# Routing of layer one: from a stage of its own into the loop of context attention, in a two-layer decoder on one Trainium2 core

## Chip, cores and metric

One NeuronCore of one Trainium2 chip. The metric is the device time of one execution in microseconds (us). TensorE (PE; its weight loads are PEld), VectorE (DVE), ScalarE (ACT), GpSimd (POOL) and SyncE (SP, which only issues transfers) run their own instruction streams and wait for each other on semaphores.

## The reference, cut to what matters

A decoder of two layers on x (16 sequences of 112 tokens, width 256) and a context (16 x 375 x 256). Each layer is self-attention, attention to the context and a mixture of experts, each added to x. The part in question is the routing of layer one, on the normalised output of its context attention:

```python
x = x + _L1_xattn_ref(_layernorm(x), ctx_1024, ...)      # 8 heads of 64, 375 context tokens
x = x + _L1_ffn_ref(_layernorm(x), ...)
# in _L1_ffn_ref, for each sequence (Tt = 112, E = 8, K = 2, cap = 33):
logits = jnp.einsum('btc,ce->bte', x, router_w) + router_b
top_k_logits, expert_indices = jax.lax.top_k(logits, K)
expert_probs = jax.nn.softmax(top_k_logits, axis=-1)
ei = jnp.swapaxes(expert_indices, 0, 1).ravel()          # all first choices, then all second ones
one_hot = jax.nn.one_hot(ei, E, dtype=jnp.int32)
pos = jnp.cumsum(one_hot, axis=0) * one_hot - 1          # the rank of a token within its expert
buf = jnp.zeros((E, expert_capacity, Cc), x.dtype)
expert_inputs = buf.at[ei.ravel(), pos.ravel()].add(xr)  # out of the capacity: dropped
# then silu(h * g) @ w_c_proj per expert, and each token collects its two outputs by expert_probs
```

## The kernel before, in words

`decoder` runs the stages one after another: `linear_attention`, `add_and_norm`, `context_attention_0`, `experts_0`, `self_attention_1`, `context_attention_1`, `experts_1`. Each is a block in which every engine has its own program; between blocks the engines meet, and a finished stage clears its semaphores.

`context_attention_1` (line 1888) works a sequence at a time. Turn i of all engines' loops does the attention of sequence i, whose heads come in two groups of four: scores, maximum (DVE, L2060), exponentials (ACT, L2004), transposes of the probabilities (PE, L2219), their copy out of PSUM (DVE L2066 and ACT L2010 in turn), the products with the values (PE, L2236). Between these main steps stand side steps, which prepare the sequences ahead (context two turns ahead; keys, values, queries one ahead) and finish the one behind (`result`, `rows`). A table, `side = Side([...])`, gives each a sequence offset and one of two PSUM banks, one emptied by ACT and one by DVE, and the order of the table is that of TensorE and of the engine that empties the bank. Each engine's order is written out in its `iteration`; no scheduler changes it. `sequences_ahead` runs turns -3 to 0 unrolled, 1 to 12 in a loop of two turns, 13 to 16 unrolled. DVE normalises the rows of sequence i - 1 in turn i (`rows_ready`, L2097) and writes them a second time to `XN` (L2098); `rows` transposes them to `xnT`.

`experts_1` (line 2275) then has four blocks. The first routes all sequences at once: 32 router matmuls (L2318), the two best experts by `top_two` on DVE, ranks by products with an upper triangle of ones (L2323 to L2325), probabilities, positions; SP loads the weights of experts 0 and 1. The second makes for each sequence, on DVE, the one-hot matrix of its 8 x 33 slots, and multiplies the rows with it in fp32 (L2424) to `ex`, the expert inputs, already transposed. The third is the experts' work: weights and inputs are split in a high and a low fp32r half (ACT rounds, L2486; GpSimd subtracts, L2475) and multiplied in three products (`split_products`). The fourth combines.

`experts_0` works through BLOCKS = 44 tiles of 128 rows, which hold every distribution of 3584 rows over 16 experts padded to tiles.

## Time and profile before

| | |
|---|---|
| median of 3 runs | 1944.72 us (1944.21 to 1952.29) |
| the profiled execution | 1952.73 us |
| its span, first to last instruction | 1951.1 us |
| mean granted clock of TensorE | 0.946 of full |
| busy: PE, DVE, ACT, POOL | 1719.9, 1177.2, 828.2, 452.9 us |
| context attention of layer one, first scores to the last rows | 1184.1 to 1552.6 us |
| routing and slots | 1552.6 to 1609.0 us |
| experts of layer one | 1609.0 to 1901 us |

The span is the time of one execution between its first and last instruction; the rest of the 1952.73 lies around it. Times in rows count from the span's start. In a timeline row, "[0.36 <-PE ps L1215]" says that the engine had been idle for 0.36 us and what ended that. "x8" merges neighbouring instructions; an fp32 matmul shows as two records, an fp32r one as one.

### The profile page before, as it was taken

What the parts mean: (1) busy time and instruction counts of PE and PEld (TensorE: products, weight loads), DVE (VectorE), ACT (ScalarE), POOL (GpSimd) and SP (SyncE); (2) the same over time, 40 slices, a digit from 0 to 9 for tenths busy, and PEclk for the clock granted to TensorE, in tenths of its full rate; (3) what the DMA queues carried; (4) which work ended last, traced back from release to release, by engine and by line L of the source; (5) the groups of instructions that cost most, each with busy time, mean ns of one, the idle gap of its engine ahead of it and who ended that gap; (6) DMA issues with size and microseconds to landing.
All of it is one profiled execution on the core that took longest, in us unless ns stands there. A gap on an engine that the chain in (4) does not pass through costs nothing. (4 is left out here: it accounts for less than half of the span.)

```text
span 1951.1 us, 39011 instructions
## 1 busy us (share of the span) xinstructions
PE 1719.9 (88%) x13070; PEld 1375.2 (70%) x13070; DVE 1177.2 (60%) x2667; ACT 828.2 (42%) x2420; POOL 452.9 (23%) x710
## 2 busy tenths in 40 slices
PE   3887689999998687799999949999999759999998
PEld 2555456666666476688888837777787649999996
DVE  3887546777777443366666534666665365666657
ACT  1332345555555123244444424444444245554534
POOL 1111201222222222212112021111111006544523
PEclk9999789999999699799999969999999879999999
DMA  8000133333350433000000000000000122312101
GB/s 241 0 0 0 55 93 125 119 123 123 123 171 11 151 119 120 20 11 13 11 9 12 4 24 24 17 16 16 21 10 1 40 90 70 126 66 93 37 1 38
DMA packets 87656, 114.20 MB, mean 59 GB/s; under 512 B 4832, under 2 KB 77071, under 8 KB 87311
## 3 DMA queue, kind: packets, MB, share of 16 engines
q1 hardware_dynamic: 82382, 99.91, 16.0%
q0 software_dynamic: 5184, 13.11, 2.0%
q8 instruction: 54, 0.88, 0.2%
q14 instruction: 36, 0.29, 0.1%
HBM read 65.04 MB, written 47.97 MB: 58 GB/s over the span
## 5 line engine op out<-in xcount | busy, mean ns | idle before, releaser
L1215 PE MATMUL ps<-e_ex_high,e_w_high 128*128 128x264 f32 x512 | 146.8, 287 | 5.4 <-POOL e_w_low L2475 5.4
L1215 PE MATMUL ps<-e_ex_high,e_w_low 128*128 128x264 f32 x512 | 146.5, 286 | 0.0
L1215 PE MATMUL ps<-e_ex_low,e_w_high 128*128 128x264 f32 x512 | 146.2, 286 | 0.0
L931 ACT ACTIVATE c_probs<-ps,c_negmax 112x375 f32<-112x375 f32 x256 | 143.7, 581 | 2.1 <-DVE c_negmax L1028 2.1
L1028 DVE TENSOR_REDUCE c_negmax<-ps 112x2 f32<-112x750 f32 x128 | 114.2, 934 | 34.7 <-PE ps L1152 34.7
L1814 PE MATMUL ps<-xnT,s_qkv 128*128 (+1 forms) x1024 | 130.5, 285 | 2.0 <-DVE xnT L1661 1.0
L1121 PEld LDWEIGHTS ps<-const,c_probs 112*125 112x125 f32 x768 | 99.0, 193 | 45.3 <-DVE c_pT L1044 19.4
L1814 PEld LDWEIGHTS ps<-xnT,s_qkv 128*128 128x128 f32 x1024 | 123.2, 199 | 6.4 <-DVE xnT L1661 1.7
L1628 ACT ACTIVATE s_probs<-ps,s_negmax 112x112 f32<-112x112 f32 x256 | 86.7, 365 | 74.8 <-DVE s_negmax L1677 74.8
L1121 PE MATMUL ps<-const,c_probs 112*125 112x112 f32 x768 | 115.1, 287 | 3.5 <-DVE c_pT L1044 2.0
L2004 ACT ACTIVATE c_probs<-ps,c_negmax 112x375 f32<-112x375 f32 x128 | 71.7, 574 | 83.1 <-DVE c_negmax L2060 83.1
L1215 PEld LDWEIGHTS ps<-e_ex_high,e_w_high 128*128 128x128 f32 x512 | 97.6, 191 | 5.8 <-issue 5.8
L1215 PEld LDWEIGHTS ps<-e_ex_high,e_w_low 128*128 128x128 f32 x512 | 97.6, 191 | 0.0
L1215 PEld LDWEIGHTS ps<-e_ex_low,e_w_high 128*128 128x128 f32 x512 | 97.5, 190 | 0.0
L2475 POOL TENSOR_TENSOR e_w_low<-e_wgt,e_w_high 128x256 fp32r<-128x256 f32 x64 | 49.0, 766 | 175.4 <-ACT e_w_high L2486 175.4
L2495 ACT ACTIVATE xnT<-ps,columns 128x528 f32<-128x528 f32 x64 | 45.0, 703 | 99.6 <-PE ps L1215 99.6
L2536 DVE SCALAR_TENSOR_TENSOR xnT<-ps,columns,xnT 128x528 f32<-128x528 f32 x64 | 49.0, 766 | 60.4 <-PE ps L1215 60.4
L919 ACT COPY c_pT<-ps 125x672 f32<-125x672 f32 x64 | 46.0, 719 | 84.2 <-PE ps L1121 84.2
L2542 DVE CAST e_hid_high<-xnT 128x528 fp32r<-128x528 f32 x64 | 45.3, 708 | 58.1 <-ACT xnT L2501 47.7
L2060 DVE TENSOR_REDUCE c_negmax<-ps 112x2 f32<-112x750 f32 x64 | 57.1, 934 | 36.0 <-PE ps L2207 34.2
L1215 PE MATMUL ps<-e_hid_high,e_w_high 128*128 128x264 f32 x256 | 73.6, 287 | 5.9 <-DVE e_ex L2523 4.2
L2219 PE MATMUL ps<-const,c_probs 112*125 112x112 f32 x384 | 65.8, 281 | 7.9 <-DVE c_pT L2066 3.1
(361 smaller groups left out, 4600.2 us busy)
## 6 DMA issues: line engine op xcount, KB each, us to landing
expert_rows<-d_zero SPq DMA_DIRECT2D x16, 2240.0 KB, 12.1
c_ctx_in<-in_ctx SPq DMA_DIRECT2D x32, 375.0 KB
e_wgt<-in_L_ffn_w_gate SPq DMA_DIRECT2D x8, 1024.0 KB, 5.0
e_wfc<-in_L_ffn_w_c_fc SPq DMA_DIRECT2D x8, 1024.0 KB, 7.2
e_wpj<-in_L_ffn_w_c_proj SPq DMA_DIRECT2D x8, 1024.0 KB, 9.6
e_x_in<-expert_rows SPq DMA_DIRECT2D x44, 128.0 KB, 2.0
expert_rows<-e_y POOLq DMA_DIRECT2D x44, 128.0 KB, 2.0
s_qkv<-in_L_attn_W_qkv SPq DMA_DIRECT2D x1, 3072.0 KB, 11.2
```

What stands on the lines that cost most here:

```text
L919: nc.scalar.copy(pT[:, 2:4, :], ps[:KC, BANK_PT:BANK_PT + 2, 0:SC]).then_inc(pT_ready, 1)
L931: last = nc.scalar.activation(probs[:, g % 2, r, :], ps[:T, r, 0:S], ACT.Exp, bias=negmax[:, par, h:h + 1], accum_out=sums[:, par, h:h + 1])
L1028: nc.vector.tensor_reduce(negmax[:, par, h:h + 3:2], ps[:T, 2 * piece:2 * piece + 2, 0:S], AX.X, ALU.max, negate=True).then_inc(max_done, 1)
L1121: last = nc.tensor.transpose(ps[:KC, BANK_PT + r % 2, k * T:(k + 1) * T], probs[:, g % 2, r, k * KC:(k + 1) * KC], ident[:T, :T])
L1215: last = nc.tensor.matmul(out, a, b, start=start and n == 0, stop=stop and n == len(pairs) - 1)
L1628: last = nc.scalar.activation(probs[:, j, a, :], ps[:T, BANK_S + j, a * T:(a + 1) * T], ACT.Exp, scale=0.125, bias=negmax[:, h:h + 1], acc ...
L1814: last = nc.tensor.matmul(bank[:, u4 * T:(u4 + 1) * T], wv[:, c, j, n * 128:(n + 1) * 128], sh.xnT[:, c, i + 1, :], start=(c == 0), stop=( ...
L2004: nc.scalar.activation(probs[:, x, :], ps[:T, x, 0:S], ACT.Exp, scale=0.125, bias=negmax[:, h:h + 1], accum_out=sums[:, h:h + 1]).then_inc ...
L2060: nc.vector.tensor_reduce(negmax[:, h:h + 2], ps[:T, 2 * pair:2 * pair + 2, 0:S], AX.X, ALU.max, negate=True).then_inc(max_done, 1)
L2219: last = nc.tensor.transpose(ps[:KC, BANK_PT, k * T:(k + 1) * T], probs[:, x, k * KC:(k + 1) * KC], ident[:T, :T])
L2475: last = nc.gpsimd.tensor_tensor(low, whole, high.bitcast(F32), ALU.subtract)
L2536: nc.vector.scalar_tensor_tensor(ubuf[:, j % 2, :, :], ps[:, 0:2, 0:HALF], sh.columns[:, bass.ds(n_all, 1)], gbuf[:, :, :], ALU.add, ALU.m ...
```

## The change

The routing of layer one moves into the turns of `context_attention_1`. A class `Dispatch1` holds its steps; q is the sequence:

- turn q + 1: DVE normalises the rows once (`dispatch.xn`; `XN` is gone), casts their high half (`keep_high`), GpSimd makes the low half (`keep_low`). `rows` becomes `rows_ranks`, stands earlier (after the first transposes of group 1) and copies to `own`; `inverse` becomes `inverse_logits` and has the router's two matmuls behind it.
- turn q + 2: best two experts (`take_best`, `mark_experts`), GpSimd keeps the two best values; the rank products behind the row transposes of the next sequence in `rows_ranks`; DVE masks them (`take_ranks`) and selects slots (`select_slots`); GpSimd builds the one-hot matrix in fp32r (`one_hot`: two multiplications and an addition on 112x264).
- turn q + 3: the side steps `slots0` and `slots1`, behind the scores of either group, each two fp32r matmuls of 264 columns (high and low half of the rows); ACT copies to `ex`.

`sequences_ahead` now unrolls turns -3 to 4, loops over 5 to 12, and unrolls 13 to 19. The first two blocks of `experts_1` are gone. Expert 0's weights are loaded at the start of the attention on SP, behind the first two context loads; expert 1's at the start of the experts' block. The probabilities are computed in the third piece of the experts (ACT's exponential ahead of the first). BLOCKS becomes 43. The rest makes room in SBUF: `self_attention_1` keeps its tiles in the memory of layer zero's expert weights, and tiles that only the start of the kernel needs are freed before `context_attention_0`.

```diff
-BLOCKS = 2 * ROWS // TILE + E0
+BLOCKS = (2 * ROWS - E0) // TILE + E0
...
-    for i in range(-ahead, 1):
+    start = 5 if behind else 1
+    for i in range(-ahead, start):
...
+class Dispatch1:
...
+    def take_best(self, dve, q, u, taken):
...
+        self.link(dve, q, 1, nc.vector.max(self.best[:, u, :], self.values[:, :]))
+        nc.vector.max_index(self.best_at[:, :], self.best[:, u, :], self.values[:, :]).then_inc(self.best_ready, 1)
...
+    def mark_experts(self, dve, q):
...
+        self.link(dve, q, 2, nc.vector.tensor_copy(self.chosen[:, :], self.best_at[:, 0:2]))
+        nc.vector.tensor_tensor(self.sh.hot[:, q, :, :], mid(self.sh.c("expert_ids")[:T, 0:E1], 2), bc(self.chosen[:, :], E1),
+                                ALU.is_equal).then_inc(self.hot_ready, 1)
...
+    def rank_products(self, pe, bank, q):
+        nc = self.nc
+        pe.wait_ge(self.hot_ready, q + 1)
...
+    def select_slots(self, dve, q, taken):
...
+        self.link(dve, q, 3, nc.vector.tensor_reduce(self.sh.slot[:, q, :], self.ranks[:, :, :], AX.X, ALU.add))
...
+            last = nc.vector.tensor_scalar(self.sel[:, k, :], self.sh.c("slots")[:T, :], self.sh.slot[:, q, k:k + 1], None, ALU.is_equal)
...
+    def slot_products(self, pe, bank, q, u, c):
+        nc = self.nc
+        pe.wait_ge(self.oneh_ready, q + 1)
+        pe.wait_ge(self.low_ready, q + 1)
+        for n, part in enumerate((self.xn_high, self.xn_low)):
...
-    side = Side([("result", -1, ON_DVE), ("query", 1, ON_ACT), ("key0", 1, ON_DVE), ("context0", 2, ON_ACT),
-                 ("key1", 1, ON_DVE), ("key2", 1, ON_ACT),
-                 ("key3", 1, ON_DVE), ("value0", 1, ON_ACT), ("value1", 1, ON_DVE), ("context1", 2, ON_ACT),
-                 ("rows", -1, ON_DVE), ("inverse", 0, ON_DVE), ("value2", 1, ON_ACT)])
+    side = Side([("slots0", -3, ON_ACT), ("result", -1, ON_DVE), ("query", 1, ON_ACT), ("key0", 1, ON_DVE), ("context0", 2, ON_ACT),
+                 ("key1", 1, ON_DVE), ("key2", 1, ON_ACT), ("slots1", -3, ON_ACT),
+                 ("key3", 1, ON_DVE), ("rows_ranks", -1, ON_DVE, B + 1), ("value0", 1, ON_ACT), ("value1", 1, ON_DVE),
+                 ("context1", 2, ON_ACT), ("inverse_logits", 0, ON_DVE, B + 1), ("value2", 1, ON_ACT)])
...
+            load_expert(sh, sp, e1, 0, 0, e1.even)
...
-                nc.vector.tensor_scalar(sh.XN[:, i - 1, :], x, ln.mv[:T, 0:1], ln.rstd[:T, :], ALU.subtract, ALU.mult)
...
+                if within(i - 2):
+                    dispatch.mark_experts(dve, i - 2)
                 maxima(i, 1)
+                if within(i - 1):
+                    dve.wait_ge(xn_ready, i)
+                    dispatch.keep_high(dve, i - 1, 1 - par, slots_used(i))
                 evacuate("key3", i, par)
                 copy_probs(i, 1, 0)
+                evacuate("rows_ranks", i, par)
                 context_statistics(i + 3, 1 - par)
+                if within(i - 2):
+                    dispatch.select_slots(dve, i - 2, (side_done[ON_DVE], side.done("rows_ranks", i)))
                 inverse_sums(i)
                 evacuate("value1", i, par)
                 copy_probs(i, 1, 2)
-                evacuate("rows", i, par)
-                evacuate("inverse", i, par)
+                evacuate("inverse_logits", i, par)
...
+                load_expert(sh, sp, w, 1, 1, w1)
...
+                        if is_first and n == 2:
+                            probabilities()
```

VectorE, from the copy of the last keys to the copy that frees the last transposes. Before, in the loop, where rows that set registers (REGISTER_ALU, ISA) stand among the others:

```order
L2112 BN_AGGR c_ctx_mean_var<-c_ctx_stats 125x2 x3
L80 REGISTER_ALU
L2114 TENSOR_SCALAR c_ctx_var_eps<-c_ctx_mean_var 125x3
L2070 ISA
L2071 RECIPROCAL c_inv<-c_sums 112x8
L2073 COPY c_inv_wide<-c_inv 112x512
L2040 ISA
L2049 COPY c_v<-ps 125x512
L2065 REGISTER_ALU
L2066 COPY c_pT<-ps 125x336
```

Now, in turn 4, which is unrolled:

```order
L1966 CAST d_xn_high<-d_xn 112x256
L2191 COPY c_kT<-ps 128x375
L2206 COPY c_pT<-ps 125x336
L2185 COPY d_own<-ps 128x224
L1948 TENSOR_TENSOR d_ranks<-ps,hot 112x16
L2246 BN_STATS c_ctx_stats<-c_ctx_in 125x6 x3
L2252 BN_AGGR c_ctx_mean_var<-c_ctx_stats 125x2 x3
L2254 TENSOR_SCALAR c_ctx_var_eps<-c_ctx_mean_var 125x3
L1955 TENSOR_REDUCE slot<-d_ranks 112x2
L1960 TENSOR_SCALAR d_sel<-const,slot 112x33 x2
L2211 RECIPROCAL c_inv<-c_sums 112x8
L2213 COPY c_inv_wide<-c_inv 112x512
```

The copy of the transposed rows and the masking of the ranks stand ahead of the context statistics now, and the reduction and the two selections between the statistics and the sums; `c_v` and `c_pT` follow as before.

TensorE, from the second last transposes of group 1 to the last side step. Before, in turn 13 (`c_probs` are the probabilities, `c_cn` the context, `c_xn` the rows, `c_inv_wide` the inverse sums):

```order
L2219 MATMUL ps<-const,c_probs 125x112 x3
L2182 MATMUL ps<-const,c_cn 128x125 x3
L2172 MATMUL ps<-const,c_xn 128x112 x2
L2219 MATMUL ps<-const,c_probs 125x112 x3
L2163 MATMUL ps<-const,c_inv_wide 128x112 x4
```

Now, in turn 4:

```order
L2377 MATMUL ps<-const,c_probs 125x112 x3
L2340 MATMUL ps<-const,c_cn 128x125 x3
L2377 MATMUL ps<-const,c_probs 125x112 x3
L2314 MATMUL ps<-const,c_inv_wide 128x112 x4
L1911 MATMUL ps<-e_router,d_own 112x8 x2
```

The row transposes have gone from between the last two groups of transposes (they stand ahead of the values now, with the rank products behind them), and the router's matmuls follow the inverse sums.

## Rows read from the trace of the kernel before

**Rows 1.** Engine windows: stretch, its length, busy of PE, PEld, DVE, ACT, POOL, granted clock, DMA share, GB/s.
```profile
1206.41:1229.20 22.79, 22.55 (x168) 18.03 (x168) 14.53 (x33) 10.74 (x28) 4.01 (x5) 1.00 0.06 19
...
1548.00:1567.00 19.00, 14.36 (x74) 13.47 (x74) 2.60 (x8) 0.00 (x0) 0.55 (x1) 0.64 0.63 226
```

**Rows 2.** Timeline of one loop turn: start us, us, engine, line, operation [idle before <-releaser].
```profile
1400.11 1.52 PE L2207 MATMUL ps<-c_kT,c_qT 64*112 64x375 f32 x8
...
1401.56 0.44 PE L1215 MATMUL ps<-c_ctx_high,c_kv_high 128*128 128x376 f32 x1
...
1402.74 0.40 PEld L2219 LDWEIGHTS ps<-const,c_probs 112*125 112x125 f32 x3 [0.19 <-ACT c_probs L2004]
...
1403.78 1.07 DVE L2106 BATCH_NORM_STATS2 c_ctx_stats<-c_ctx_in 125x6 f32<-125x256 f32 x3
...
1405.45 0.20 DVE L2071 RECIPROCAL c_inv<-c_sums 112x8 f32<-112x8 f32 x1
...
1406.48 0.69 DVE L2049 COPY c_v<-ps 125x512 f32<-125x512 f32 x1 [0.36 <-PE ps L1215]
...
1407.09 0.50 DVE L2066 COPY c_pT<-ps 125x336 f32<-125x336 f32 x1
...
1407.73 0.55 PE L2219 MATMUL ps<-const,c_probs 112*125 112x112 f32 x3
...
1422.90 1.52 PE L2207 MATMUL ps<-c_kT,c_qT 64*112 64x375 f32 x8
```

**Rows 3.** Timeline, from the loop's last rows to the first expert matmul.
```profile
1552.19 0.41 DVE L2097 TENSOR_SCALAR c_xn<-X,c_mean_var,c_rstd 112x256 f32<-112x256 f32 x1 [0.66 <-POOL c_rstd L113]
...
1553.17 0.39 DVE L2047 COPY xnT<-ps 128x224 f32<-128x224 f32 x1 [0.24 <-PE ps L2172]
...
1554.48 12.08 PE L2318 MATMUL ps<-e_router,xnT 128*112 128x8 f32 x64 [1.35 <-PEq L98]
...
1574.60 0.39 DVE L2380 TENSOR_SCALAR e_sel<-const,e_pos 112x33 f32<-112x33 f32 x2 [0.53 <-PEq L2307]
...
1603.68 0.67 ACT L2404 COPY e_ex<-ps 128x264 f32<-128x264 f32 x2 [0.86 <-PE ps L2424]
...
1604.70 0.40 ACT L2486 CAST e_w_high<-e_wgt 128x256 fp32r<-128x256 f32 x1 [0.35 <-PEq L2387]
...
1609.02 0.56 PE L1215 MATMUL ps<-e_ex_high,e_w_high 128*128 128x264 f32 x1 [5.38 <-POOL e_w_low L2475]
```

**Rows 4.** Timeline, GpSimd and VectorE side by side, layer one and layer zero.
```profile
1405.60 0.87 POOL L1949 TENSOR_TENSOR c_ctx_rstd<-c_ctx_var_eps,const 125x3 f32<-125x3 f32 x1 [6.54 <-DVE c_ctx_var_eps L2114]
...
1405.69 0.43 DVE L2073 COPY c_inv_wide<-c_inv 112x512 f32<-112x512 f32 x1
...
342.20 0.23 DVE L712 TENSOR_SCALAR d_hot<-const,d_chosen 112x16 f32<-112x16 f32 x1
...
657.59 0.73 POOL L729 TENSOR_TENSOR X<-X,d_xn 112x256 f32<-112x256 f32 x1
...
657.86 0.50 DVE L712 TENSOR_SCALAR d_hot<-const,d_chosen 112x16 f32<-112x16 f32 x1 [0.15 <-DVE d_chosen L711]
```

**Rows 5.** Timeline of TensorE: layer zero's gate and ranks, expert matmuls.
```profile
560.96 0.56 PE L649 MATMUL ps<-e_gate,d_own 128*112 128x16 f32 x4 [0.38 <-DVE c_v L976]
...
561.57 0.35 PE L654 MATMUL ps<-d_totals,const 112*112 112x16 f32 x2
...
1616.02 0.28 PE L1215 MATMUL ps<-e_ex_high,e_w_low 128*128 128x264 f32 x1
...
1616.14 0.29 PE L1215 MATMUL ps<-e_ex_high,e_w_high 128*128 128x264 f32 x1
```

**Rows 6.** Timeline of TensorE in the experts of layer zero, two blocks.
```profile
702.43 0.59 PE L1473 MATMUL ps<-e_down,e_hidT 128*128 x2
...
704.06 0.59 PE L1473 MATMUL ps<-e_down,e_hidT 128*128 x2
```

**Rows 7.** Page, DMA issues: operation, count, KB each, us to landing.
```profile
e_wpj<-in_L_ffn_w_c_proj SPq DMA_DIRECT2D x8, 1024.0 KB, 9.6
```

More of the change, by code:

```diff
@@ L44, in constant_columns @@
     put("count16", np.tile(np.arange(16, 0, -1), (T, 1)))
-    put("slots", np.tile(np.arange(CAP), (T, 1)))
+    put("slots", np.tile(np.arange(1, CAP + 1), (T, 1)))
     put("upto", np.triu(np.ones((T, T))))
@@ L1491, in __init__ @@
     def __init__(self, steps):
-        self.steps = steps
-        self.bank = {name: u for name, _, u in steps}
-        self.offset = {name: offset for name, offset, _ in steps}
+        self.steps = [step if len(step) == 4 else step + (B,) for step in steps]
+        self.bank = {name: u for name, _, u, _ in self.steps}
+        self.offset = {name: offset for name, offset, _, _ in self.steps}
+        self.times = {name: times for name, _, _, times in self.steps}
     def present(self, name, i):
-        return within(i + self.offset[name])
+        k = i + self.offset[name]
+        return not isinstance(k, int) or 0 <= k < self.times[name]
     def before(self, name, i):
         total, later = 0, 1
-        for other, offset, u in self.steps:
+        for other, offset, u, times in self.steps:
             if other == name:
@@ L1516, in within, with sequences_ahead, self_attention_1 @@
     return not isinstance(q, int) or 0 <= q < B
-def sequences_ahead(eng, ahead, iteration):
-    for i in range(-ahead, 1):
+def sequences_ahead(eng, ahead, iteration, behind=0):
+    start = 5 if behind else 1
+    for i in range(-ahead, start):
         iteration(i, i % 2)
-    with eng.Fori(1, B - 4, 2) as i:
+    with eng.Fori(start, B - 4, 2) as i:
         iteration(i, 1)
         iteration(i + 1, 0)
-    for i in range(B - 3, B + 1):
+    for i in range(B - 3, B + 1 + behind):
         iteration(i, i % 2)
-def self_attention_1(nc, sh, w):
+def self_attention_1(nc, sh, w, spare):
     H, DH, HALF = 16, 64, 4 * T
@@ L2159, in aside @@
                     pe.wait_ge(side_done[u], taken)
-                if name == "inverse":
-                    pe.wait_ge(inv_ready, i + 1)
-                    for c in range(4):
-                        last = nc.tensor.transpose(bank[:, c * T:(c + 1) * T],
-                                                   inv_wide[:, 2 * c:2 * c + 2, :].rearrange("p h d -> p (h d)"), ident[:T, :T])
+                if name == "inverse_logits":
+                    if within(i):
+                        pe.wait_ge(inv_ready, i + 1)
+                        for c in range(4):
+                            last = nc.tensor.transpose(bank[:, c * T:(c + 1) * T],
+                                                       inv_wide[:, 2 * c:2 * c + 2, :].rearrange("p h d -> p (h d)"), ident[:T, :T])
+                    if within(i - 1):
+                        last = dispatch.logits(pe, logits_at)
                 elif name == "result":
@@ L2354, in experts_1 @@
+        ex = sh.ex
+        held = sb("held", [T, B, 2])
+        prob = sb("prob", [T, 2, B])
+        diff = sb("diff", [T, B])
+        diff_ready, ediff_ready, chain = sem("diff_ready"), sem("ediff_ready"), sem("chain")
+        w1 = ExpertWeights(lambda name, shape: sb(name + "_odd", shape))
+        weights, w_in = (w.even, w1), w.w_in
         sel = sb("sel", [T, 2, CAP])
@@ L2359, in experts_1 @@
         spare = lambda at, n: flat_xnT[:, at:at + n]
-        own = spare(10 * HALF, 2 * D)[:T].rearrange("p (u d) -> p u d", u=2)
         def sequences(eng, step):
@@ L2526, in take_outputs, with probabilities @@
                     last.then_inc(out_taken, 1)
+                def probabilities():
+                    link = chained(dve, chain, 0)
+                    nc.vector.tensor_scalar(held[:, :, :], sh.slot[:, :, :], float(CAP), None, ALU.min)
+                    dve.wait_ge(ediff_ready, 1)
+                    link(nc.vector.tensor_scalar(prob[:, 0, :], prob[:, 1, :], 1.0, None, ALU.add))
+                    link(nc.vector.reciprocal(prob[:, 0, :], prob[:, 0, :]))
+                    link(nc.vector.tensor_tensor(prob[:, 1, :], prob[:, 1, :], prob[:, 0, :], ALU.mult))
                 def pair(e2, is_first, is_last):
```

334 lines of the change are left out of this document (177 added, 157 removed).

## The prediction

> **What bounds the kernel now.** The chain of waits that ended last reaches back only into the combining of the outputs, so I read the stages instead: the engine windows for context attention of layer one, the timeline for what follows it, and the timeline of one turn of the loop. In the loop TensorE is busy 22.55 of 22.79 us, at the full granted clock [rows 1]; one sequence takes 22.79 us, from second scores to second scores (1400.11 to 1422.90) [rows 2]. TensorE is the bound, but inside the turn it waits for VectorE in one place: between 1403.78 and 1407.59 VectorE works almost without a gap (statistics, sums, copy of values, copy of probabilities), and the transposes of the last head start at 1407.73, when that last copy is there [rows 2]. After the loop comes the stage the change is about. The last normalised rows are finished at 1552.60 (1552.19 + 0.41), the first real expert matmul starts at 1609.02 [rows 3]. In these 56.4 us nothing overlaps with attention: 64 router matmul records, top-two, ranks, and 16 small slot products; TensorE's granted clock is 0.64 in the first 19 us of it [rows 1].
>
> **What goes.** All of these 56.4 us as a stage of its own. What replaces them is a tail: the last sequence's router, ranks and slots still hang behind its rows. Laid end to end from 1552.60: rank products of sequence 14, copy of the own rows, logits, best two, marking: about 4 us, since these are small instructions of 0.2 us on VectorE [rows 4] and pairs of 0.2 to 0.4 us on TensorE [rows 5], which at half clock take twice that. TensorE then stands before the slots of sequence 14, which wait for GpSimd's one-hot (three instructions on 112x264; its 112x256 add took 0.73 [rows 4], so 2.3 with the hand-overs), then twice product and ScalarE copy (0.4 each; a pair of 264-column copies took 0.67 [rows 3]): about 3.8 us. Then ranks, selection (1.5), one-hot (2.3) and two products with copies (1.9) of sequence 15. Sum 13 to 13.5 us; bounds 10 (sequence 14 hidden entirely) and 18 (every hop at half clock, GpSimd held). I take 13. Behind it stay the way from one block to the next with the clearing of semaphores, 0.9 (after the loop's last copy, to the router's first matmul, an estimate: the row copy ended at 1553.56, and the router began at 1554.48 [rows 3]), and the splitting of the first expert piece, 4.3 (1604.70 to 1609.02 [rows 3]). New stage 18.2 us; gain 38.2.
>
> One block less in the experts of layer zero (43 for 44): the same matmul group starts at 702.43 and 704.06, so 1.6 us [rows 6]. The stage of layer zero is a chain of such blocks on TensorE, so all of it counts.
>
> **What the loop gains in work, TensorE.** Per sequence: logits, two fp32 matmuls of 8 columns; layer zero's gate and ranks with 16 columns are the nearest, three of them from 560.96 to 561.57, so 0.20 each [rows 5] and 0.40 for the pair. Ranks, two more: 0.40. Slot products, now four fp32r matmuls of 264 columns: 0.12 each (1616.02 to 1616.14) [rows 5], 0.50, in two pairs. Together 1.3 us on an engine that has 0.24 to spare in 22.79. The row transposes only move.
>
> **What the loop gains in waits, VectorE.** The order fence shows what now stands ahead of the copy that TensorE waits for: the copy of the own rows (about 0.4; 0.50 was for 336 columns [rows 2]), the masking of the ranks (0.2), their reduction (0.2), two selections (0.39 for two [rows 3]). The write of XN falls away, but it stood where VectorE waited for the scores anyway; best two and marking sit in such gaps too, and the high half of the rows is cast while TensorE makes the last keys. So these cost nothing, and if that cover were gone each would cost 0.2 to 0.5 per turn. With 0 at the start of the second scores (1400.11), after the change: TensorE has scores to 1.45 (1401.56), slots to 1.70, keys to 2.73 (1.18 less the 0.19 that the next transposes waited [rows 2]), transposes at 2.93 (the slot copy stands 0.35 ahead of the exponentials on ScalarE), rows and ranks from 3.65 (they wait for the copy of the keys, about 0.5 like the other copies) to 4.27; VectorE has rows and ranks out at 5.1, statistics at 6.8 (1.67, from 1403.78 to 1405.45), selection 7.45, sums 8.1, values 8.8, probabilities 9.3; TensorE resumes at 9.4, where before it did at 7.62 (1407.73) [rows 2]. That is +1.78. Logits add 0.40, the first slot pair 0.25, and a hand-over of some 0.1 goes, since the inverse transposes no longer wait for the row copy. One turn grows by 2.3 us, to 25.1. Bounds: 1.3 (TensorE's work alone) and 3.8.
>
> Then the selections. The instruction right behind the statistics is GpSimd's power, 0.87 us on the inverse deviations [rows 4]. The selections are issued some 0.2 us after it starts. Two rows speak. Beside that very power instruction VectorE's wide copy took 0.43 us, no longer than always [rows 4]: not held. But layer zero's comparison with constants, 0.23 us usually, took 0.50 when it began 0.27 us after a GpSimd add of 0.73, and ended 0.04 after it [rows 4]: held to its end. The selection is of the second kind. The Trainium skill ("SBUF — State Buffer", section on the two separate sides) says of this that GpSimd and a VectorE instruction in a two-port mode share one port pair under a lock that is kept for a whole instruction; by that rule the selections are held, and a selection that isn't two-port would pass. Held, the first selection ends at 0.95 after the statistics (0.87 and the hand-over) instead of at about 0.45, so 0.5 us a turn more; I take it, because the comparison is the nearer row. Bounds 0 and 0.7.
>
> Sum over the turns, not held: turn 1 has logits alone (1.3 with its copies), turn 2 ranks too (2.0), turns 3 to 12 have 2.3 each (23.0), 13 and 14 no statistics any more (1.9 each), turn 15 little (1.1): 31.2 us. Held: 11 turns of 0.5, 5.5 more: 36.7.
>
> **Edits at nothing or nearly.** Expert 0's weights are loaded at the start of the attention, behind the first two context loads in SP's queue and ahead of the third; the third is needed some 20 us later, and such a load lands in 9.6 us [rows 7]. Expert 1's is issued only when the expert block starts; ScalarE wants it at the third piece, some 13 us later, against 9.6 [rows 7] for the last part. If this cover is thin, 1 to 3 us. The probabilities (four small VectorE instructions, and a minimum) sit in the third piece of the experts, beside a GpSimd that is never idle there: 0 to 1, taken as 0.5. Nothing else is on an end.
>
> **Sum.** +36.7 - 38.2 - 1.6 + 0.5 = -2.6 us. The profiled execution took 1952.7 for a span of 1951.1, 8.0 above the median of the runs shown (1944.7); I apply the difference to the median: **1942 us**. A measurement here can tell about 0.5% (9.7 us) from no change, so this is within it: the stage is gained and the loop takes it back.
>
> **The rivals.**
> Not held: the selections pass beside GpSimd. 31.2 - 38.2 - 1.6 + 0.5 = -8.1: 1936.6. For it: the wide copy; against: the comparison.
> TensorE's work alone: VectorE's stretch gets shorter elsewhere or I laid it too pessimistically, and a turn costs 15 x 0.4 + 14 x 0.4 + 13 x 0.5 = 18.1 in all. -21.2: 1923.5. Against it is that the last copy already sets a start today [rows 2], and 1.25 us are put ahead of it.
> Slower: VectorE's queue in that stretch becomes the bound of the whole turn. Everything that lengthens it between the statistics and the probability copy is paid one for one by TensorE, in about 12 turns. The new steps bring about ten semaphore and register steps, and both selections, the masking and the cast can be held in turn by GpSimd. It decides from 1.5 us a turn above my unheld 2.3 (-8.1 + 12 x 1.5 = +9.9). At 1.8 it gives +13.5: 1958. For it: the rows of the held comparison; against: most small instructions of layer zero's loop, with the same kind of GpSimd work beside them, keep 0.2 us.
> The change does not do what it says: the tail does not shrink, because TensorE meets each of the last three turns with a wait of several us. Each sequence more than one that is exposed costs 6 us: about 1948.
>
> **How the numbers follow.** Forecast 0.40; not held 0.22; TensorE's work alone 0.15; VectorE's queue as bound 0.14; tail or a load that collides 0.09. The likeliest case has its own range, 1935 to 1950, by the bounds of the tail and of one turn. For 8 in 10 the range has to reach the other cases: 1923 to 1958. Faster by over 0.5% (below 1935.0): all of the third case, near half of the second, a tenth of the first: 0.33. Slower by over 0.5% (above 1954.4): most of the fourth, a bit of the first and last: 0.17. Between: 0.50.
>
> **What would show it.** Right: a turn of 25.4 to 25.8 (22.79 now); the transposes of the last head waiting 1.2 to 1.8 us for the probability copy; the first selection at about 0.8 us where it would take 0.2, ending with the power instruction; TensorE busy near 92% of a turn; from the last rows to the first expert matmul 17 to 19 us. Wrong: a turn near 24.1 (TensorE's work alone) or above 26.2 (the queue as bound); GpSimd's one-hot running into the context rows; a wait of ScalarE for expert 1's weights; a granted clock below 1.00 in the loop.

## The result, and the profile after

Median 1946.65 us (1930.59 to 1951.91, 13 runs); the kernel before, on the same chip, 1952.29 us (1944.21 to 1960.81, 13 runs). The ratio is 0.9949, with a 95% interval of 0.9927 to 0.9972; a second series of the same kernel gave 0.9942 (0.9918 to 0.9965). So the change takes off 10 to 11 us, half a per cent, and both intervals leave out 1. The ratio is not the quotient of the two medians, which would be 0.9971. Every ratio below leaves out slow executions (among the changed kernels one of experiment 1, 9070.51 us). The profiled execution took 1935.13 us for a span of 1933.5; TensorE's mean granted clock was 0.957.

The sum, piece by piece, from the two profiles (the ends of a piece are the scaled outputs of a sequence, written by VectorE, and the experts' matmuls):

| piece | before | after | difference |
|---|---|---|---|
| tiles of layer zero's experts, first to last output product | 75.0 | 73.1 | -1.9 |
| first scaled output to the last (15 turns) | 340.8 | 365.1 | +24.3 |
| last scaled output to the first expert matmul | 61.8 | 26.2 | -35.6 |
| first to last expert matmul | 290.6 | 290.5 | -0.1 |
| from there to the end (combining) | 51.5 | 54.3 | +2.8 |

That gives -10.5 us. The rest by which this one profile is ahead (7 us in layer zero, before and behind the tiles) is spread between executions: over all profiles below of kernels with 43 tiles, the first scaled output lies between 1190.7 and 1203.7 us. Much of that spread has one place. Layer zero's attention to the context, from its first scaled output to its last, takes 404.8 to 405.0 us in five of the fourteen profiles on record (this one among them; mean granted clock 0.974 or 0.975) and 409.8 to 412.2 us in the other nine (the profile of before among them; 0.943 to 0.954). No edit here touches that stage.

One turn of the loop after the change, from the timeline of the kernel as changed (start, duration, engine, line, operation, idle time before it and what ended that); it answers to [rows 2]:

```profile
1403.21 0.79 POOL L2085 TENSOR_TENSOR X<-X,c_bo 112x256 f32 x1
1403.32 0.70 DVE L1933 CAST d_chosen<-d_best_at 112x2 f32<-112x2 uint32 x1
...
1405.05 1.52 PE L2365 MATMUL ps<-c_kT,c_qT 64*112 64x375 f32 x8
...
1406.50 0.39 PE L1998 MATMUL ps<-d_oneh,d_xn_high 112*128 112x264 f32 x1
1406.73 0.28 PE L1998 MATMUL ps<-d_oneh,d_xn_low 112*128 112x264 f32 x1
...
1409.26 0.48 PE L1202 MATMUL ps<-c_kv_high,c_ctx_high 128*125 128x512 f32 x1
...
1411.39 0.17 DVE L2254 TENSOR_SCALAR c_ctx_var_eps<-c_ctx_mean_var 125x3 f32<-125x3 f32 x1
...
1411.62 0.17 DVE L1955 TENSOR_REDUCE slot<-d_ranks 112x16 f32 x1
1411.64 0.86 POOL L2074 TENSOR_TENSOR c_ctx_rstd<-c_ctx_var_eps,const 125x3 f32<-125x3 f32 x1 [2.86 <-DVE c_ctx_var_eps L2254]
...
1412.06 0.39 DVE L1960 TENSOR_SCALAR d_sel<-const,slot 112x33 f32<-112x33 f32 x2 [0.27 <-DVE slot L1955]
...
1412.93 0.68 DVE L2189 COPY c_v<-ps 125x512 f32<-125x512 f32 x1
1413.53 0.50 DVE L2206 COPY c_pT<-ps 125x336 f32<-125x336 f32 x1
1413.94 0.66 ACT L2126 ACTIVATE c_ctx_high<-ps,columns 128x375 fp32r<-128x375 f32 x1
1414.17 0.55 PE L2377 MATMUL ps<-const,c_probs 112*125 112x112 f32 x3 [0.91 <-DVE c_pT L2206]
...
1414.58 0.74 POOL L1991 TENSOR_TENSOR d_oneh<-d_part 112x264 fp32r<-112x264 f32 x1 [0.49 <-POOL d_part L1985]
1415.28 0.85 POOL L2079 TENSOR_TENSOR c_ctx_low<-c_ctxT,c_ctx_high 128x375 fp32r<-128x375 f32 x1
```

With the second scores as zero (1405.05), the last transposes start at 9.12 us; before it was 7.62, the forecast said 9.4. The two selections take 0.39 us together in the middle of GpSimd's power instruction (1411.64 to 1412.50): they are not held. In the same turn GpSimd's addition does hold something: the cast of two numbers, 0.16 us usually, takes 0.70 beside it and ends 0.02 behind it. That lies in idle time. The last two rows show GpSimd's one-hot running into its context work: the low half of the context starts 0.68 us after its high half is there (1414.60), where before it was under 0.1. TensorE waits for neither. A full turn is 24.76 us (22.81 before).

Windows of a full turn and of the stretch from the last scaled output to the first expert matmul, in the kernel as changed (columns as in [rows 1]):

```profile
1245.10:1269.80 24.70, 23.82 (x180) 19.31 (x180) 15.73 (x43) 11.41 (x30) 7.00 (x10) 1.00 0.05 17
1562.45:1588.68 26.23, 8.64 (x35) 6.42 (x35) 8.11 (x30) 6.69 (x21) 8.76 (x14) 0.63 0.13 42
```

TensorE is busy 23.82 of 24.70 us, 96%, where I had said 92%: it got more work (1.27 us) than idle time (0.64 us). The timeline of the tail, which answers to [rows 3]:

```profile
1568.11 0.41 DVE L2238 TENSOR_SCALAR d_xn<-X,c_mean_var,c_rstd 112x256 f32<-112x256 f32 x1
...
1573.75 0.56 PE L1998 MATMUL ps<-d_oneh,d_xn_high 112*128 112x264 f32 x1 [2.91 <-issue]
...
1575.60 0.41 PE L1941 MATMUL ps<-hot,const 112*112 112x16 f32 x2
...
1580.24 0.56 PE L1998 MATMUL ps<-d_oneh,d_xn_high 112*128 112x264 f32 x1 [3.86 <-issue]
...
1582.34 0.39 ACT L2003 COPY ex<-ps 128x264 f32<-128x264 f32 x1 [0.90 <-PE ps L1998]
1584.28 0.41 ACT L2548 CAST e_w_high<-e_w_gate_even 128x256 fp32r<-128x256 f32 x1 [1.56 <-PEq L98]
...
1588.68 0.56 PE L1202 MATMUL ps<-e_ex_high,e_w_high 128*128 128x264 f32 x1 [6.38 <-POOL e_w_low L2537]
```

From the last rows (1568.52) to the last slot copy it is 14.2 us (forecast 13), from there to the next block's first cast 1.55 (0.9), then 4.4 (4.3): 20.2 in all, for the 56.4 of before.

### The profile page after: what moved, and what is told of

It reads as the page before. It is cut to its first block and busy times, and to the rows that moved or that the text cites. A ratio compares the mean times of both kernels' runs of the same rounds, so it can differ in the third digit from the quotient of the medians.

```text
span 1933.5 us, 39095 instructions
## 1 busy us (share of the span) xinstructions
PE 1697.0 (88%) x13119; PEld 1363.6 (71%) x13119; DVE 1168.2 (60%) x2727; ACT 822.5 (43%) x2402; POOL 498.7 (26%) x789
## 5 line engine op out<-in xcount | busy, mean ns | idle before, releaser
L1121 PEld LDWEIGHTS ps<-const,c_probs 112*125 112x125 f32 x768 | 95.9, 188 | 45.5 <-DVE c_pT L1044 20.5
L1121 PE MATMUL ps<-const,c_probs 112*125 112x112 f32 x768 | 111.8, 282 | 4.8 <-ACT c_probs L931 2.5
L2377 PE MATMUL ps<-const,c_probs 112*125 112x112 f32 x384 | 65.0, 278 | 19.1 <-DVE c_pT L2206 14.9
L2377 PEld LDWEIGHTS ps<-const,c_probs 112*125 112x125 f32 x384 | 56.5, 188 | 31.8 <-issue 18.0
```

The costliest lines, as they stand in the source:

```text
L1121: last = nc.tensor.transpose(ps[:KC, BANK_PT + r % 2, k * T:(k + 1) * T], probs[:, g % 2, r, k * KC:(k + 1) * KC], ident[:T, :T])
L2377: last = nc.tensor.transpose(ps[:KC, BANK_PT, k * T:(k + 1) * T], probs[:, x, k * KC:(k + 1) * KC], ident[:T, :T])
```

## The experiments

All are edits of the changed kernel unless it is said otherwise. Ratios are against the kernel before, run beside them.

### 1. The slot selection later

```diff
                 context_statistics(i + 3, 1 - par)
-                if within(i - 2):
-                    dispatch.select_slots(...)
                 inverse_sums(i)
                 evacuate("value1", i, par)
                 copy_probs(i, 1, 2)
+                if within(i - 2):
+                    dispatch.select_slots(...)
```

> Edit: the slot reduction and the two slot selections move from behind the statistics to behind VectorE's last probability copy, 0.9 us of work with its hand-overs. Stage figures are from the profile; a turn of the changed kernel is 24.76 us (22.79 before the change), and its last transposes wait 0.91 us for that copy. Theory A (the wait for VectorE's queue is the part of the turn's growth that is not TensorE's work): the copy comes 0.8 to 0.9 us earlier, the wait falls to under 0.2, the turn to 23.9 to 24.1 us, and the time falls by 12 x 0.75 = 9 us against the changed kernel. Rival B (the turn is set by TensorE's own work, and the 0.91 us would only turn up at another wait): the turn stays within 0.2 us of 24.76. Rival C (the selection is now late for GpSimd, whose one-hot runs into the context work): the one-hot ends under 0.5 us before the slot products need it, or the inverse copy moves; the turn is above 24.3.

Ratio 0.9932 (0.9909 to 0.9955). The turn is 24.5 us (mean of turns 3 to 12: 24.51, as changed 24.75): 0.25 shorter, so neither A's 0.75 nor quite B. C's sign is there, since the one-hot now holds up GpSimd's context work by 2.6 to 2.8 us, but TensorE waits for none of it: in the loop its only listed wait is still the one for `c_pT`. The timeline shows why the turn hardly shrinks:

```profile
1396.91 1.52 PE L2365 MATMUL ps<-c_kT,c_qT 64*112 64x375 f32 x8
...
1403.60 0.43 DVE L2213 COPY c_inv_wide<-c_inv 112x512 f32<-112x512 f32 x1
...
1404.09 0.39 PE L1202 MATMUL ps<-c_kv_high,c_ctx_low 128*125 128x512 f32 x1
...
1404.52 0.69 DVE L2189 COPY c_v<-ps 125x512 f32<-125x512 f32 x1 [0.50 <-PE ps L1202]
1405.13 0.50 DVE L2206 COPY c_pT<-ps 125x336 f32<-125x336 f32 x1
...
1405.78 0.55 PE L2377 MATMUL ps<-const,c_probs 112*125 112x112 f32 x3 [0.65 <-DVE c_pT L2206]
```

Of the 0.83 us taken out of VectorE's stretch, 0.50 turn up as a wait of the value copy for TensorE's products. It waited for them before the change as well, 0.36 us [rows 2]. So VectorE's queue was only 0.33 us of what set this point in the changed kernel, and nothing of it before; the rest were TensorE's value products, and the change moved them 1.24 us back. (From the second scores, the value copy could start at 6.37 before, 1406.48 less 1400.11, and starts at 7.61 here, 1404.52 less 1396.91.) Slots (0.35) and row transposes with ranks (0.57) now stand ahead of them, and the waits between. The row "waits for c_pT" names only the last link.

The rows explain most of the wait that is left, too. In the kernel before, the transposes of the rows filled TensorE's time while the two copies ran:

```profile
1406.04 0.40 PE L1215 MATMUL ps<-c_kv_high,c_ctx_low 128*125 128x512 f32 x1
...
1407.22 0.41 PE L2172 MATMUL ps<-const,c_xn 112*128 112x112 f32 x2
```

From the end of the last value product to the last transposes it is 1.29 us before (1406.44 to 1407.73) and 1.30 here (1404.48 to 1405.78). The way over the two copies hasn't changed; the 0.5 us of row transposes that stood in it have gone to a place ahead of the products. That is read from the rows; no run puts them back.

### 2. The last ranks ahead of the slots of sequence 14

```diff
                 scores(i, par, 0)
+                last_ranks = isinstance(i, int) and i == B + 1
+                if last_ranks:
+                    aside("rows_ranks", i, par)
                 aside("slots0", i, par)
...
                 transposes(i, 1, 0)
-                aside("rows_ranks", i, par)
+                if not last_ranks:
+                    aside("rows_ranks", i, par)
```

> Edit: in turn 17 alone TensorE does the rank products of the last sequence ahead of the slot products of sequence 14, where the changed kernel has them behind (1575.60, though their marks are there at 1572.98). Theory A (the tail is one chain through TensorE's order): ranks 2.5 us earlier, and with them selection, one-hot and last slots; from the last rows to the first expert matmul 17.8 us instead of 20.2, the total 2.4 us less, which the timed runs will hardly tell. Rival B (GpSimd's one-hots are the chain of the tail, since both sequences' pass through it): less than 0.8 us off. The turns stay 24.76.

```profile
1563.13 0.41 DVE L2238 TENSOR_SCALAR d_xn<-X,c_mean_var,c_rstd 112x256 f32<-112x256 f32 x1
...
1568.15 0.52 PE L1941 MATMUL ps<-hot,const 112*112 112x16 f32 x2 [1.92 <-DVE hot L1934]
...
1570.56 1.22 POOL L1985 TENSOR_TENSOR d_part<-hot,d_sel 112x264 f32<-112x264 f32 x2 [1.76 <-DVE d_sel L1960]
...
1574.99 0.39 ACT L2003 COPY ex<-ps 128x264 f32<-128x264 f32 x1 [0.90 <-PE ps L1998]
...
1581.34 0.56 PE L1202 MATMUL ps<-e_ex_high,e_w_high 128*128 128x264 f32 x1 [6.38 <-POOL e_w_low L2541]
```

From the last rows (1563.54) to the first expert matmul 17.8 us, as A said; 2.4 off. GpSimd still waits 1.76 us for the selection, so its one-hots are not the chain. The ratio, 0.9937 (0.9908 to 0.9967), can't tell 2.4 us, and this profile had a stall in the experts, which the next section turns to.

### 3. TensorE's added work twice

```diff
+        for again in range(2):
             for c in range(2):
                 last = nc.tensor.matmul(bank, self.own[:, c, :], self.w.router[:, c, :], ...)
...
-        for n, part in enumerate((self.xn_high, self.xn_low)):
+        for n, part in 2 * list(enumerate((self.xn_high, self.xn_low))):
```

with the late selection of experiment 1.

> Edit: as in the run with the late selection, and the router products and all four slot products are issued twice (the second time from start again, so the result is the same). My forecast priced a single set at 0.40 and 0.50 us a turn, one for one. Theory A (with the wait gone TensorE is the bound, so its work is paid in full): the turn is 0.9 us longer than with the late selection alone, about 24.9; if the four fp32r products of 264 columns cost 0.12 each. Rival B (part of this work lies in waits that TensorE has anyway): under 0.5 us longer.

Ratio 1.0021 (0.9987 to 1.0055), turn 25.38: 0.87 us over experiment 1, where A said 0.9. TensorE's work is paid one for one, and the sum of the forecast's two prices (0.40 and 0.50) holds; the run doesn't part them. With 0.4 for the ranks, which no run doubled, 1.3 of the turn's 1.95 us is TensorE's own work, as its busy time says (+1.27).

### 4. One tile of layer zero back

```diff
-BLOCKS = (2 * ROWS - E0) // TILE + E0
+BLOCKS = 2 * ROWS // TILE + E0
```

> Edit: layer zero's experts work through 44 tiles again instead of 43, all else as changed. Theory A (a tile is a link of a chain on TensorE): 1.6 us more between the first and the last tile of that stage, and nothing else moves. Rival B (the 7.4 us by which the profile of the changed kernel is ahead in layer zero beyond that come with the tile count): the stages of layer zero fall back by 9 us. If neither, those 7.4 us are spread between executions and show up here with either sign. The combining at the end, 2.7 us longer than before though not touched, is 50.8 us from the last expert product if it comes with the kernel's code, or returns to 48.1 if it is spread between executions.

Ratio 0.9954 (0.9927 to 0.9982). From the first to the last output product of the tiles it is 74.8 us, with 43 tiles 73.1, 73.0 and 72.7 (as changed, its second profile, experiment 2). A holds: 1.7 to 2.1 us for a tile by these (72.7 to 73.3 us over all profiles with 43 tiles). The profile came out at 1195.7 us to the first scaled output, earlier than the changed kernel's: the 7.4 us are spread. The combining took 52.4 us here, 53.4 to 54.3 in the other profiles of the changed kernel and its edits, 51.5 and 51.8 in the two of the kernel before (the second with the wait of number 7). What of the 2.8 us belongs to the change isn't settled.

### 5 to 8. A stall in the experts that both kernels have

In the profiles of all four kernels above, and not in the changed kernel's, the first cast of a hidden piece on VectorE looks like this (experiment 1, timeline; the rows after it are GpSimd's, whose subtractions split the weights):

```profile
1590.51 7.93 DVE L2614 CAST e_hid_high<-xnT 128x528 fp32r<-128x528 f32 x1 [1.19 <-ACT xnT L2563]
1590.59 0.74 POOL L2537 TENSOR_TENSOR e_w_low<-e_w_fc_even,e_w_high 128x256 fp32r<-128x256 f32 x1
...
1597.42 0.73 POOL L2537 TENSOR_TENSOR e_w_low<-e_w_proj_even,e_w_high 128x256 fp32r<-128x256 f32 x1
...
1598.48 0.71 DVE L2615 TENSOR_TENSOR e_hid_low<-xnT,e_hid_high 128x528 fp32r<-128x528 f32 x1
...
1599.24 0.59 PE L1202 MATMUL ps<-e_hid_high,e_w_high 128*128 128x264 f32 x1 [7.79 <-DVE e_hid_low L2615]
```

The same place in the kernel as changed:

```profile
1595.38 1.11 DVE L2614 CAST e_hid_high<-xnT 128x528 fp32r<-128x528 f32 x1 [1.30 <-ACT xnT L2563]
1595.47 0.74 POOL L2537 TENSOR_TENSOR e_w_low<-e_w_fc_even,e_w_high 128x256 fp32r<-128x256 f32 x1
```

The cast came 0.08 and 0.09 us ahead of GpSimd's next subtraction. Once it got past after one of them, once it was held through eleven in a row, to 0.3 us behind the last. TensorE's windows around it in experiment 1 show the second cost, the granted clock after the idle stretch:

```profile
1588.00:1592.00 4.00, 3.45 (x29) 1.00 0.31 96
1592.00:1596.00 4.00, 0.00 (x0) 0.76 0.00 0
1596.00:1600.00 4.00, 0.76 (x3) 0.50 0.17 16
1600.00:1604.00 4.00, 4.00 (x20) 0.50 0.97 389
```

With no work at all it fell to 0.50 and was still there in the next 4 us, fully busy. From the first to the last expert matmul it is 299.0 to 299.6 us with the stall in these four, 290.5 without. Three theories, four kernels on one chip; number 5 is the changed kernel once more, 6 adds a wait to it, 7 adds the same wait to the kernel before, 8 has the edits of 1, 2 and 6 together.

```diff
+                def pieces(e2):
                     for n in range(2 * NJ):
                         j = n % NJ
+                        if not (isinstance(e2, int) and n < 4):
+                            pool.wait_ge(hid_ready, e2 * NJ + n - 3)
                         pool.wait_ge(piece_rounded, e2 * NJ + n + 1)
...
+                pieces(0)
+                with pool.Fori(2, E1 - 1, 2) as e2:
+                    pieces(e2)
```

The edit also writes out GpSimd's first two experts ahead of its loop; no run has that alone.

> Edit: none; the changed kernel once more, for a second profile beside the others on one chip. In the four experiments before this one VectorE's first cast of a hidden piece in the last experts took 7.93 us (TensorE idle 7.8 us behind it), in the profile of the changed kernel 1.11 us, at the same place and with the same work around it. Theory A (whether the cast gets past GpSimd's unbroken row of subtractions is decided by some tens of nanoseconds and falls either way from execution to execution): this profile shows either 1.1 or 7.9 us, and if 7.9, then 299 us from the first to the last expert matmul instead of 290.5. Rival B (the stall came in with the edits of those four kernels): 1.1 us again.

> Edit to the changed kernel: in the last experts GpSimd's subtractions for piece n wait until the low half of hidden piece n - 4 is done, so that it is idle when VectorE's first cast comes. Theory A (the cast is held as long as GpSimd works without a gap): the cast takes 0.4 to 0.7 us, 290 to 291 us from the first to the last expert matmul in every profile, and the timed runs fall by up to 8.7 us against the changed kernel, by the share of its executions that have the stall. Rival B (the added wait makes GpSimd late for TensorE): the same cast is short, but TensorE waits for the low halves of the weights and the stage is above 293 us. Rival C (the cast is long for another reason, such as the weight transfer that lands at the same time, 1.04 of the queues' share): it stays at 7.9.

> Edit to the kernel BEFORE the change: the same wait of GpSimd, all else as before. In its profile the cast took 0.66 us. Theory A (the stall belongs to the experts' code that both kernels share, and fell in some executions of the kernel before too, whose times lie in two groups 10 us apart): faster than before by 2 to 8 us in the median, and the upper group of times gone or thinned. Rival B (only the changed kernel meets the phase in which the cast is held): the same time as before within 0.15%, and then the change has brought a cost of its own, to be set against its gain.

> Edits to the changed kernel: late selection, rank products first in turn 17, and GpSimd's wait in the experts, together. Sum of the single ones: turns 24.50 as in the run with the late selection (3 us), tail 3 us, experts 8.5 us in the executions with the stall: against the kernel before 0.987 to 0.990 of its time if theory A of the stall holds, 0.992 if it doesn't.

| | ratio to before | longest cast of a hidden piece | first to last expert matmul |
|---|---|---|---|
| 5, as changed | 0.9942 (0.9918 to 0.9965) | 1.10 | 290.5 |
| 6, with the wait | 0.9919 (0.9887 to 0.9952) | 0.59 | 286.0 |
| 7, before, with the wait | 0.9941 (0.9917 to 0.9964) | 0.58 | 286.0 |
| 8, all three | 0.9871 (0.9833 to 0.9908) | 0.58 | 286.3 |

The cast in number 6, and the first subtraction behind it:

```profile
1603.67 0.44 DVE L2620 CAST e_hid_high<-xnT 128x528 fp32r<-128x528 f32 x1 [0.71 <-ACT xnT L2569]
...
1604.93 0.74 POOL L2539 TENSOR_TENSOR e_w_low<-e_w_gate_even,e_w_high 128x256 fp32r<-128x256 f32 x1 [1.95 <-DVE e_hid_low L2621]
```

Number 5 rules out nothing alone: its profile had no stall. Together with 9 to 11 below it does: of nine profiles of kernels with the changed kernel's code for the experts and without the wait, six had the stall and three not, the kernel as changed twice among the three and an edited one (number 11) once. So not every edit brings the stall. But no kernel was profiled once with it and once without, and what decides is open. The cast starts 0.06 to 0.10 us ahead of GpSimd's next subtraction in the six, and 0.04, 0.08 and 0.53 in the three (numbers 5, the kernel as changed, 11). What speaks for a change from execution to execution is the spread: the kernel as changed ran in 1932.06 to 1950.38 us in number 5's series, with the wait in 1932.84 to 1938.55 (12 and 6 runs).

Numbers 6 and 7 show what holds the cast: where GpSimd has a gap (1.95 us in the rows above) it takes 0.44 us. Theory B of number 6 falls, since TensorE waits for no low half that it didn't wait for before (6.4 us once, at the start, in both). Theory C falls, since the cast is short, and since the DMA share was 0.00 in four of the microseconds through which it was held (1592 to 1596 above). The wait gives more than it was made for: 4.6 us even against executions without a stall. The later casts show where. As changed, 30 of the 64 take over 0.9 us beside a subtraction, and TensorE's listed waits for them and for the inputs come to 7.4 us; with the wait no cast takes over 0.59, and the waits are 2.4.

And it is no matter of the change: the kernel before gains 11 us from it by the timed runs. The changed kernel gains 4 to 5 (0.9919 against 0.9942), with intervals that overlap. With the wait in both kernels (numbers 6 and 7) the change itself is worth 4 us by the ratios, 6 by the means of 6 and 12 runs, and the two profiles differ by 9. So its gain with the stall out of play isn't settled better than some 3 to 9 us. The longer time of the kernel before in stalled executions was never in my sum, since the one profile of it had none. Number 8 came in at the lower end of its expectation (0.987 to 0.990).

### 9 to 11. What GpSimd holds

Number 9 moves GpSimd's addition; 10 and 11 have selections on 34 columns, beside the power and beside the addition.

```diff
                     pool.wait_ge(ctx_var, q + 1)
+                    add_bias(q - 3)
                     nc.gpsimd.tensor_tensor(rstd[:, :], veps[:, :], ..., ALU.pow)
...
-                add_bias(i)
+                if not within(i + 3):
+                    add_bias(i)
...
-        self.sel = sb("sel", [T, 2, CAP])
+        self.sel = sb("sel", [T, 2, CAP + 1])
```

> Edit to the changed kernel: GpSimd's bias addition (112x256, 0.79 us) is moved from the start of the turn to just ahead of its power instruction, both behind the context statistics, so that VectorE's two slot selections (33 columns) now fall beside an addition and no longer beside the power. In the changed kernel the pair takes 0.39 us beside the power. Theory A (GpSimd's addition holds small VectorE instructions and its power does not, as the cast of two columns beside an addition, 0.70, and the comparison of layer zero suggest): the first selection or the reduction ahead of it ends with the addition, and from the start of the reduction to the end of the selections it is over 1.2 us instead of 0.83. Rival B (an odd number of columns keeps the selection from being held by anything): the same 0.83 as beside the power.

> Edit to the changed kernel: the selections work on 34 columns instead of 33 (the last one is not read), beside the power as in the changed kernel. Theory A (what matters is GpSimd's instruction, the power holds nothing): 0.39 us for the pair again. Rival B (the odd width is why they passed): the pair ends with the power, 0.7 us or more.

> Edit to the changed kernel: both edits, selections on 34 columns beside GpSimd's addition. Theory A (the addition holds): over 1.2 us from the start of the reduction to the end of the selections. Under rival B (width) also held; if neither the odd nor the even one is held, my held comparison of layer zero had another cause.

Group of one line in a stretch of full turns (count, then duration in ns as minimum, median, maximum), as changed, then number 9, then 10, then 11:

```profile
L1960 DVE TENSOR_SCALAR d_sel<-const,slot x24: 233/241/244, 1238.8 to 1510.1; 112x33 f32<-112x33 f32 x24
```

```profile
L1960 DVE TENSOR_SCALAR d_sel<-const,slot x24: 230/240/572, 1233.5 to 1507.4; 112x33 f32<-112x33 f32 x24
```

```profile
L1960 DVE TENSOR_SCALAR d_sel<-const,slot x24: 232/240/243, 1243.8 to 1515.1; 112x34 f32<-112x34 f32 x24
```

```profile
L1960 DVE TENSOR_SCALAR d_sel<-const,slot x24: 229/240/572, 1245.2 to 1519.1; 112x34 f32<-112x34 f32 x24
```

A turn of number 9:

```profile
1408.11 0.73 POOL L2086 TENSOR_TENSOR X<-X,c_bo 112x256 f32 x1 [2.98 <-DVE c_ctx_var_eps L2256]
1408.41 0.61 DVE L1960 TENSOR_SCALAR d_sel<-const,slot 112x33 f32<-112x33 f32 x2 [0.27 <-DVE slot L1955]
1408.80 0.86 POOL L2075 TENSOR_TENSOR c_ctx_rstd<-c_ctx_var_eps,const 125x3 f32<-125x3 f32 x1
```

Beside the power no selection is held, at either width. Beside the addition the first of the pair is held at either width, in eleven of the twelve turns that the group covers: 0.46 to 0.57 us for 0.24, to 0.03 or 0.04 us behind the addition's end. The second, which then falls beside the power, takes 0.23. A of all three in its direction; the size was off: from the reduction to the end of the selections it is 1.04 us (1407.98 to 1409.02), not over 1.2. The turn grows to 25.0 (0.23). One profile and one time each, so there is no ratio. What makes the power let the selection pass isn't shown: it differs from the addition in its operation and in its size, 3 columns for 256, and no run parts the two.

### 12. The probability copy ahead of the value copy

The kernel of number 8, with

```diff
-                evacuate("value1", i, par)
                 copy_probs(i, 1, 2)
+                evacuate("value1", i, par)
```

> Edit to the kernel with all three edits: VectorE copies the probabilities of the third head (which TensorE's last transposes wait for) ahead of value1 instead of behind it. With the late selection that wait is still 0.65 us, and VectorE stands idle 0.5 us before the value copy, waiting for TensorE's products. Theory A (what is left of the wait is the order value copy, probability copy, gated by TensorE's own products, not the length of VectorE's queue): the last transposes come 0.25 to 0.35 us earlier; but the value copy is then 0.45 later, and the inverse transposes behind it wait for its bank, so the turn is 24.3 to 24.6 us, at most 0.2 shorter. Rival B (the queue): no earlier start of the last transposes at all.

Ratio 0.984 (0.9813 to 0.9867), median 1924.68: about 31 us off the kernel before. TensorE waits for the copy 4.4 us in twelve turns instead of 7.8, and the turn is 24.42. A holds, in both halves: the copy is earlier, and little of it is left at the turn's end. Its interval and that of number 8 overlap, so the timed runs tell each from the changed kernel, but not from the other.

## Why the prediction was right and where it was wrong

The forecast was 1942 us from a sum of -2.6, the measured ratios mean -10 to -11 from the same median, some 1934 us. The time of the runs lies well in the range, but the change was called "within 0.5%" and came out at 0.51 and 0.58%, too near that line to call. The rival "not held" (-8.1) is the one that came true in its mechanism. That its number fits as well is partly luck: the turns cost 6.9 us less than it has, the tail 2 more, the combining 2.8 that stand in no term, and the stall in the experts, also in no term, is in the timed runs of both kernels by shares that nobody measured. A small slip in the chances changes nothing here: the parts named for "faster by over 0.5%" add up to some 0.30 and not 0.33.

- **The selections held, +5.5: wrong.** "The selection is of the second kind" was the step that failed. The two rows differed in GpSimd's instruction, an addition on one side and the power on the other, and I read the difference on VectorE's side. The row taken at the very same power instruction [rows 4] was the nearer one. Experiments 9 to 11 show it: addition yes, power no, width no matter. And held, the selections cost 0.23 us a turn (number 9), not 0.5. The Trainium skill ("SBUF — State Buffer", section on the two separate sides) has any GpSimd instruction that comes first hold the ports; the trace agrees for the addition, and disagrees for the power (0.39 us in the midst of its 0.86).
- **TensorE's work, 1.3 us a turn: right** (experiment 3: 0.87 for 0.9; busy +1.27).
- **TensorE resumes at 9.4: nearly right, by a wrong path.** It was 9.12. I laid VectorE's queue end to end; in fact the value copy waits for TensorE, whose products my list moved too. VectorE's queue costs 0.25 a turn (experiment 1), and the wait that is left, 0.65, is the way over the two copies behind TensorE's products, which the row transposes used to fill by 0.5. "The row transposes only move" put that at nothing. A turn grew by 1.95 for 2.3.
- **31.2 us over the turns, not held: 24.3.** Of the 6.9 missing, 3.5 are ten turns of 0.35; 1.1 the first two (0.86 and 1.32 for 1.3 and 2.0), 0.2 the next to last ones; 1.9 is turn 15, 20.85 us here but 20.3 to 24.2 in the other profiles. It runs partly at half clock, which my sum had as work alone.
- **The tail, 18.2 for 20.2:** 1.2 in the chain (at half clock, TensorE's ranks stood behind the slots of sequence 14, which experiment 2 prices at 2.4), 0.65 in the way to the next block.
- **One tile, 1.6: right, or a little low** (1.7 to 2.1). **The probabilities, 0.5: nothing** (290.5 and 290.6); GpSimd holds them, but TensorE doesn't wait. **Expert 1's weights at 1 to 3 if thin: nothing.** ScalarE doesn't wait for them.
- **Not in the sum:** the combining, +2.8 in this pair of profiles, and its cause is open. And the stall in the experts: the profile of before had none, but executions of that kernel that had it would go with the 11 us that the wait gives it. They don't explain its spread of 17 us alone: with the wait its twelve times still fall into 1938.18 to 1941.69 and 1944.63 to 1947.80, and the attention of layer zero, 7 us shorter in some profiles than in others, is another such switch. How often each kernel has the stall was not measured; if the shares differ, part of the ratio is luck of phase and not the change.

Signs: of the "right" ones, the wait of 1.2 to 1.8 us (0.91), the held selection, the turn of 25.4 to 25.8, the 92% and the 17 to 19 us of the tail failed; of the "wrong" ones one came, GpSimd's one-hot running into the context rows (by 0.68 us, and nothing waited for it). The clock in the loop was 1.00.

## What to carry to other kernels

When a copy is added to a queue, ask first what the instruction behind it waits for now: 0.36 us of idle time before the value copy said that VectorE had room there and that TensorE's own order was the chain. A wait's row names the last link; take work out of that link and see how much of the wait goes. And where one engine's instruction is held by another's, look at one profile's neighbours in time, then at several profiles: a long unbroken row on GpSimd can hold a single cast of VectorE for its whole length, and a gap of one wait cost nothing that the profiles show and gave the kernel before as much as the whole change. And when work that was "only moved" leaves a place, ask what it was filling there.

## What the runs showed of the hardware

- A cast of VectorE that takes 0.44 us alone took 7.91 to 7.94 us in six of nine profiles, through an unbroken row of eleven or so GpSimd subtractions, and 0.86 to 1.11 us in the other three. It started 0.06 to 0.10 us ahead of GpSimd's next instruction in the six, 0.04, 0.08 and 0.53 in the three. The Trainium skill ("SBUF — State Buffer", section on the two separate sides) says that whichever starts first holds the ports "for the whole instruction"; here the holding went on over instruction after instruction.
- GpSimd's power on 125x3 (0.86 us) held neither a selection (0.24 each) nor a wide copy (0.43); its addition on 112x256 held a cast of two numbers to 0.70 (0.16 without it) and a selection to 0.57.
- After about 8 us without work TensorE's granted clock was 0.50 and stayed there for the next 4 fully busy us. Of the 8.7 us that the stall costs the stage, 6.3 are TensorE's longer wait for this one cast (7.8 for 1.5), and the other 2.4 go with the 4 to 5 us at half clock.
